# One held indirect transfer per recurrence step, and the low half of hs on VectorE

## The chip, the cores and the metric

The kernel runs on one core of a Trainium2 chip. The metric is the device time of one execution in microseconds (us). Three executions of the kernel before took 518.39, 520.9 and 521.04 us, a median of 520.9 us.

## The reference

For 32 sequences of 128 tokens with 256 features, the reference computes two gated blocks.

```python
# block 1: q = layernorm(x), k = v = context; 16 heads of 16
r = decay * r + kt * vt
inp = (qt * r) @ Wi.T + bi
gate = sigmoid(inp @ Wg.T + bg)
state = tanh((gate * state + (1 - gate) * inp) @ A.T + inp @ Bm.T)
out = state @ Wo.T + bo                    # x = x + tanh(g) * out
# block 2: fx = layernorm(x), 8 experts, top 2 of a softmax
shared = swiglu(fx @ w_shared_in) @ w_shared_out
hid = swiglu(fx @ w1_shared)
routed = sum over e of weight[:, e] * (hid @ w2[e])
x = x + tanh(g) * (shared + routed)
```

`state` depends on the state one token earlier, so 128 recurrence steps follow each other whatever else is done.

## The kernel before

The 128 tokens are cut into 16 tiles of 8 tokens (STEPS = 8), which for 32 sequences are 256 rows each. Five engines run programs of their own, written out by hand and held together by semaphores. Iteration i of every engine's program contains the eight recurrence steps of tile i and, in the eight slots behind them, parts of the work on neighbouring tiles: the input projections of tile i + 1, the output projection of tile i - 1, and the second block of tile i - 2. Iteration i runs from 1 to 18; the last recurrence is in iteration 15, so iterations 16 to 18 are a tail without one. Below, "step (i, t)" is step t of tile i.

One step is a ring of three engines. TensorE (PE) multiplies the high and the low half of `u` with A (L590, then L595) and raises `sum_done`. ScalarE (ACT) waits for that and computes the tanh (`tanh_step`, L959), which raises `st_ready`. VectorE (DVE) waits for that and makes `u_hi`, `u_full` and `u_lo` of the next step (`gated_state`, L1268 to L1273). Each engine runs its instructions in order, so whatever stands in a slot in front of the next step delays it if it is not done.

hs is the hidden tile of the shared expert. DVE makes it in slot 1 (L1597), ACT rounds it to the high half (L1160), and GpSimd (POOL) subtracts to make the low half (L1766), which PE needs for the product with w_shared_out in slot 3 (L576, `so_hi`, `hs_lo`). In the last tile alone, DVE makes that low half, in slot 2 (`low`, L1228).

The routed experts of tiles 0 to 11 are done in three chunks of four tiles. The rows of `hid` are kept in `hid_rows` and sent to DRAM (`hrows`), sorted by expert, by indirect DMAs that POOL issues (`scatter`, L1823, 16 a chunk, 128 rows each). When all 16 of a chunk have landed (`scattered`), SyncE (SP) issues DMA transposes that bring them back two blocks at a time (`turn_rows`, L473), PE multiplies each pair with its expert's w2 (`duo`, L623), ACT moves the product to SBUF (L1126), SP stores it to `yrows` (L483), and indirect DMAs of POOL fetch each token's rows (`gather`, L1836, 16 a chunk), which DVE adds up (L1298, L1306). Tiles 12 to 15 are dense: all eight experts for each token, in `pair` products (L576 with `hid_hi`, `hid_lo`) on PE.

AT lists the iteration and slot of each of the 36 duos, 12 a chunk; START is the iteration of each chunk's first one: 8, 12 and 15. SP issues a chunk's first four transposes at the end of its iteration START - 1; the others are issued one by one as duos are stored. POOL issues its indirect DMAs at two spots of an iteration, 0 at its start, behind a wait for tanh (i, 0), and 1 at its end, with no wait. The SCATTERS and GATHERS plans give 2 to 5 of them to a spot up to iteration 15. In between stand hs's low half, the reciprocal roots of both layernorms (`x_rstd`, L1773, and L1876) and hid's low half (L1766).

Of the kernel before, what the change touches and what calls it, by code (L numbers as in the profile page):

```python
# [50 lines left out]
STEPS = 8  # L51
# [52 lines left out]
def gated_layer(nc, x, ctx_in, g_xattn, g_ffn, Wi, bi, Wg, bg, A, Bm, Wo, bo, decay,  # L104
                w_shared_in, w_shared_out, w1_shared, w2, w_gate, gate_bias, out):
    with ExitStack() as stack:
# [276 lines left out]
        def run(eng, iteration):  # L383

            for i in range(1, LAST):
                iteration(i, first)

        AT = ([(i, slot) for i in (8, 9, 10, 12) for slot in (0, 2, 3, 5)] + [(13, slot) for slot in (0, 1, 2, 3, 5)]
              + [(14, slot) for slot in (0, 1, 2)] + [(15, 5)] + [(16, slot) for slot in range(5) for _ in range(2)] + [(16, 5)])
        DUOS = {}  # L390
        for n, at in enumerate(AT):
            DUOS.setdefault(at, []).append(n)
# [3 lines left out]
        def duo_bank(n, i, slot):  # L396

            if i < TILES:
                return bank[3 if slot == 5 and first.dense(i - 2) else {0: 5, 1: 3, 2: 5, 3: 4, 5: 5}[slot]][:, :]
            return flat(rec[n % 2][:, :, :])  # L400

        def duo_chunk(n):
# [134 lines left out]
        def _(pe):  # L537
# [256 lines left out]
            def duos_at(i, slot):  # L794

                for n in DUOS.get((i, slot), ()):
                    if n == 0:
                        pe.wait_ge(w2_lo, E)
                    if i >= TILES:
                        pe.wait_ge(st_ready, STEPS * TILES)  # L800
                        if AT[n - 2][0] >= TILES:
                            pe.wait_ge(y_ready, n - 1)
                    elif slot == 0:
                        if (i - 1, 5) in DUOS:
                            pe.wait_ge(y_ready, evacuated(i - 1, 5))
                    elif slot == 1:
                        pe.wait_ge(lg_ready, i - 1)
                    elif slot == 2:
                        pe.wait_ge(y_ready, evacuated(i, 0))
                    elif slot == 3:  # L810
                        pe.wait_ge(x1_ready, i)
                    elif first.dense(i - 2):
                        pe.wait_ge(lg_ready, i - 1)
                    else:
                        pe.wait_ge(y_ready, evacuated(i, 2))
                    duo(n, duo_bank(n, i, slot))

            def iteration(i, k):
# [103 lines left out]
                if k.has(c):  # L922
                    for q in range(len(CHUNKS)):
                        if d == last_of(q):
                            pe.wait_ge(routing, 7 * (q + 1))
                    if k.has(d):
                        pe.wait_ge(hid_ready, k.n(d))
                    else:
                        pe.wait_ge(ret_ready, k.n(1))
                    if k.dense(d):  # L930
                        pe.wait_ge(pair_used[1], k.nth(d))
                    feature_product(bank[B_SHB], "sh", xn2_s[c % 2], True, col=D).then_inc(sh_done, 1)
                    if c == 0:
                        pe.wait_ge(wide_lo, 2)
                    if k.has(a):
                        pe.wait_ge(gt_ready, k.n(a))
                    else:
                        pe.wait_ge(lg_ready, k.n(d))
                        pe.wait_ge(y_ready, evacuated(15, 5))

                    for s in range(HALVES):
                        for kc in range(KC):
                            for v in xn2_s[c % 2]:
                                last = pe.matmul(bank[B_LG][:, s * 2 * E:(s + 1) * 2 * E], v[:, kc, s * P:(s + 1) * P],
                                                 wgate_s[:, kc, :], start=(s == 0 and kc == 0 and v is xn2_s[c % 2][0]),
                                                 stop=(kc == KC - 1 and v is xn2_s[c % 2][1]), skip_group_check=True)
                    last.then_inc(lg_done, 1)
# [278 lines left out]
        def _(dve):  # L1226
# [346 lines left out]
            def iteration(i, k):  # L1573
# [44 lines left out]
                if k.has(d):  # L1618
                    dve.wait_ge(w1_done, k.n(d))
                    dve.wait_ge(sil_w_ready, k.n(d))  # L1620
                    if k.has(d - 1):
# [1 line left out]
                        dve.wait_ge(hid_lo, k.n(d - 1))  # L1623
                    dve.scalar_tensor_tensor(out=flat(hid[:, :, :]), in0=bank[B_W1B][:, :], scalar=hid_in[:, 1:2],
                                             in1=flat(sil_w[:, :, :]), op0=ALU.mult, op1=ALU.mult).then_inc(hid_ready, 1)
                if d == TILES - 1:
                    dve.wait_ge(hs_hi, k.n(d))
                    dve.wait_ge(so_done, k.n(d - 1))
                    low(flat(hs_s[1][:, :, :]), flat(hs[:, :, :]), flat(hs_s[0][:, :, :]), hs_lo)
                if k.has(f):  # L1630
                    dve.wait_ge(ln1_stats, k.n(f))
# [126 lines left out]
        def _(pool):  # L1758
# [6 lines left out]
            def low(n, whole, hi, signal):  # L1765
                pool.tensor_tensor(n, whole, hi, ALU.subtract).then_inc(signal, 1)  # L1766
# [78 lines left out]
                for row, at in zip(rows, spots, strict=True):  # L1845
                    plan.setdefault(at, []).append(row)

            spread(SCATTERS, range(0, 4), [(5, 1)] * 2 + [(6, 0)] * 3 + [(6, 1)] * 4 + [(7, 0)] * 4 + [(7, 1)] * 3)
            spread(SCATTERS, range(4, 8), [(9, 1)] * 2 + [(10, 0)] * 3 + [(10, 1)] * 4 + [(11, 0)] * 4 + [(11, 1)] * 3)
            spread(GATHERS, range(0, 4), [(12, 0)] * 4 + [(12, 1)] * 5 + [(13, 0)] * 5 + [(13, 1)] * 2)  # L1850
            spread(SCATTERS, range(8, 12), [(13, 1)] * 3 + [(14, 0)] * 4 + [(14, 1)] * 5 + [(15, 0)] * 4)
            spread(GATHERS, range(4, 8), [(15, 1)] * 4 + [(16, 0)] * 4 + [(16, 1)] * 8)
            spread(GATHERS, range(8, 12), [(17, 1)] * 16)

            def moves(i, spot):

                if spot == 0 and i < TILES and ((i, 0) in SCATTERS or (i, 0) in GATHERS):
                    pool.wait_ge(st_ready, STEPS * i + 1)
                for t, s, pick in SCATTERS.get((i, spot), ()):
                    scatter(t, s, pick)  # L1860
                for t, s, pick in GATHERS.get((i, spot), ()):
                    gather(t, s, pick)

            def iteration(i, k):
                c, d, f = i - 1, i - 2, i + 2

                moves(i, 0)
                if k.has(d) and d < TILES - 1:
                    pool.wait_ge(hs_hi, k.n(d))
                    if k.has(d - 1):  # L1870
                        pool.wait_ge(so_done, k.n(d - 1))
                    low(flat(hs_s[1][:, :, :]), flat(hs[:, :, :]), flat(hs_s[0][:, :, :]), hs_lo)
                x_rstd(f, k)
                if k.has(c):
                    pool.wait_ge(ln2_var, k.n(c))
                    pool.tensor_tensor(rs2[c % 2][:, :], ve2[c % 2][:, :], minus_half[:, :], ALU.pow).then_inc(ln2_rstd, 1)  # L1876
                    pool.wait_ge(ln2_rstd, k.n(c))
                    pool.tensor_tensor(nr2[c % 2][:, :], nm2[c % 2][:, :], rs2[c % 2][:, :], ALU.mult).then_inc(ln2_shift, 1)
                if k.has(d) and d < TILES - 1:
# [40 lines left out]
```

## Time and profile before

| | us |
|---|---|
| median of three executions | 520.9 |
| the profiled execution | 519.97 |
| its span, first to last instruction | 518.2 |
| PE busy | 434.6 (84% of the span) |
| DVE busy | 364.1 |
| ACT busy | 221.7 |
| POOL busy | 184.9 |
| mean granted TensorE clock, as a share of full speed | 0.962 |

The chain of work that ended last goes 46% through PE, 24% through DVE, 5% through ACT and 2% through POOL; 10% of it is "issue", time in which the engine waited for nothing that the profile shows, and 7% is "another core or an unknown queue", although the program runs on one core. Idle time is put down to whatever released the engine; "remote" there is a releaser that the profile could not name.

### The profile page before, as it was taken

The numbers are of one execution on the slowest core, as the hardware profiler recorded it, in microseconds if no ns is written. First come the engines' busy times: TensorE is split into PE (matmuls) and PEld (weight loads), VectorE is DVE, ScalarE is ACT, GpSimd is POOL, SyncE is SP. The second block draws the span as 40 slices with busy tenths as digits, with TensorE's granted clock in tenths as the row PEclk, the third lists the DMA queues.
The fourth block names the chain that finished last, engine by engine and source line by source line (L and its number), as shares of the span: only waits on it lengthen the run. The fifth ranks groups of instructions, "written<-read, shape, count | busy, mean of one in ns | idle before, by whom it ended". The sixth has DMA issues, their size and how long they took to land.

```text
span 518.2 us, 12156 instructions
## 1 busy us (share of the span) xinstructions
PE 434.6 (84%) x4324; PEld 355.5 (69%) x4324; DVE 364.1 (70%) x1303; ACT 221.7 (43%) x520; POOL 184.9 (36%) x225
## 2 busy tenths in 40 slices
PE   5977799999997959999988898879869979968660
PEld 4965688878885748898877777778756747645320
DVE  3687887989797857777776775767837865406865
ACT  3655555667564625464545444536232313212100
POOL 3012302224136374111154554442454370520632
PEclk9998899999999998999999999999989989979986
DMA  7783234052251221874642349647331365832424
GB/s 162 209 222 111 41 104 119 15 144 45 101 135 52 63 82 38 168 123 113 132 115 96 99 97 180 143 129 128 123 103 52 81 154 134 200 113 73 139 80 148
DMA packets 102571, 59.14 MB, mean 114 GB/s; under 512 B 74352, under 2 KB 92784, under 8 KB 102512
## 3 DMA queue, kind: packets, MB, share of 16 engines
q1 hardware_dynamic: 97776, 45.77, 36.7%
q0 software_dynamic: 4736, 12.59, 7.9%
q8 instruction: 36, 0.59, 0.5%
q14 instruction: 23, 0.19, 0.1%
HBM read 23.74 MB, written 25.56 MB: 95 GB/s over the span
## 4 chain that ended last, share of the span: by engine, by line
PE 46%; DVE 24%; issue 10%; another core or an unknown queue 7%; ACT 5%; POOL 2%; DMA 1%; POOLq 0%; DVEq 0%; ACTq 0%
PE bank L576 12%; PE bank L565 10%; PE bank L623 5%; PE rec L709 5%; PE rec L590 4%; DVE u_hi L1268 4%; PE rec L623 3%; PE rec L595 2%; DVE u_full L1270 2%; DVE r L1371 2%; PE rec L565 1%; PE bank L842 1%; ACT state L959 1%; DVE ret L1384 1%
## 5 line engine op out<-in xcount | busy, mean ns | idle before, releaser
L959 ACT ACTIVATE state<-rec 128x64 f32<-128x64 f32 x128 | 36.6, 286 | 183.6 <-PE rec L595 138.5
L1268 DVE SCALAR_TENSOR_TENSOR u_hi<-gt,state 128x64 f16<-128x64 f32 x127 | 44.6, 351 | 86.7 <-ACT state L959 73.5
L590 PE MATMUL rec<-u_hi,a_hi 128*128 128x32 f16 x512 | 48.8, 196 | 28.4 <-DVE u_hi L1268 20.5
L1836 POOL DMA_INDIRECT yg<-yrows,slots_i x48 | 49.6, 1034 | 56.0 <-issue 35.5
L1823 POOL DMA_INDIRECT hrows<-hid_rows,slots_i x48 | 49.8, 1037 | 53.6 <-issue 25.3
L590 PEld LDWEIGHTS rec<-u_hi,a_hi 128*128 128x128 f16 x512 | 37.5, 99 | 38.0 <-DVE u_hi L1268 25.9
L590 PE MATMUL rec<-u_hi,a_lo 128*128 128x32 f16 x512 | 48.3, 195 | 1.0 <-issue 1.0
L1766 POOL TENSOR_TENSOR hs_lo<-hs,hs_hi 128x512 f16<-128x512 f32 x15 | 17.4, 1163 | 72.4 <-ACT hs_hi L1160 71.6
L590 PEld LDWEIGHTS rec<-u_hi,a_lo 128*128 128x128 f16 x512 | 35.9, 99 | 3.7 <-issue 1.8
L595 PE MATMUL rec<-u_lo,a_hi 128*128 128x32 f16 x512 | 36.8, 196 | 1.5 <-issue 0.5
L565 PE MATMUL bank<-xn_hi,sh_hi 128*128 128x256 f16 x128 | 34.9, 273 | 0.0
L565 PE MATMUL bank<-xn_hi,sh_lo 128*128 128x256 f16 x128 | 34.9, 273 | 0.0
L565 PE MATMUL bank<-xn_lo,sh_hi 128*128 128x256 f16 x128 | 34.9, 273 | 0.0
L1773 POOL TENSOR_TENSOR rs<-ve,minus_half 128x2 f32<-128x2 f32 x16 | 12.3, 772 | 60.6 <-DVE nm L1439 60.6
L1270 DVE SCALAR_TENSOR_TENSOR u_full<-gt,state 128x64 f32<-128x64 f32 x127 | 33.7, 266 | 0.0
L1273 DVE TENSOR_TENSOR u_lo<-u_full,u_hi 128x64 f16<-128x64 f32 x127 | 30.4, 240 | 4.4
L576 PE MATMUL bank<-w_hi,hid_hi 128*128 128x512 f16 x64 | 25.3, 395 | 9.6 <-DVE raw_w L1289 4.1
L842 PE MATMUL bank<-whole_wo,state 128*128 128x256 f32 x128 | 32.6, 400 | 0.0
L576 PE MATMUL bank<-w_hi,xn_hi 128*128 128x256 f16 x96 | 26.3, 274 | 6.5 <-DVE hs L1597 6.2
L709 PE MATMUL rec<-cn,whole_a 128*128 128x256 f32 x128 | 31.4, 388 | 0.2 <-DVE cn L1405 0.2
L1286 DVE SCALAR_TENSOR_TENSOR raw_w<-bank,wts,raw_w 128x256 f32<-128x256 f32 x32 | 15.4, 480 | 22.7 <-PE bank L576 16.2
L595 PEld LDWEIGHTS rec<-u_lo,a_hi 128*128 128x128 f16 x512 | 23.7, 99 | 5.1 <-DVE u_lo L1273 3.2
(291 smaller groups left out, 1419.6 us busy)
## 6 DMA issues: line engine op xcount, KB each, us to landing
yrows<-squares_sh SPq DMA_DIRECT2D x18, 256.0 KB
x_sb<-in_x_dram SPq DMA_DIRECT2D x16, 256.0 KB, 3.3
c_sb<-in_ctx_dram SPq DMA_DIRECT2D x64, 64.0 KB
xr_sb<-in_x_dram SPq DMA_DIRECT2D x16, 256.0 KB
hrows<-zeros SPq DMA_DIRECT2D x4, 1024.0 KB, 5.7
yrows<-squares_w SPq DMA_DIRECT2D x15, 256.0 KB
raw_w<-in_L_ffn_w_dram SPq DMA_DIRECT2D x8, 256.0 KB, 4.4
out_dram<-raw_w SPq DMA_DIRECT2D x8, 256.0 KB
```

The lines of the kernel that those rows point to most:

```text
L565: last = pe.matmul(o, w[:, kc, at], a[:, kc, :], start=first, stop=(kc == KC - 1 and w is w_lo), skip_group_check=True)
L576: last = pe.matmul(dst, a[:, kc, s * P:(s + 1) * P], w(part, kc), start=first, stop=(kc == KC - 1 and a is a_lo), skip_group_check=True)
L590: pe.matmul(o[:, oc, :], w[:, kc, oc * P:(oc + 1) * P], u_hi[t % 2][:, kc, :], start=False, stop=False, skip_group_check=True)
L595: last = pe.matmul(o[:, oc, :], a16[0][:, kc, oc * P:(oc + 1) * P], u_lo[t % 2][:, kc, :], start=False, stop=(kc == KC - 1), skip_group_ch ...
L623: last = pe.matmul(dst[:, b * D:(b + 1) * D], hid_t[n % RING][:, half * KC + kc, b * P:(b + 1) * P], split["w2"][part][:, kc, bass.ds(e, 1 ...
L709: last = pe.matmul(rec[a % 2][:, oc, :], whole_a[:, kc, oc * P:(oc + 1) * P], cn[a % 2][:, kc, :], start=False, stop=(kc == KC - 1), skip_ ...
L842: last = pe.matmul(bank[B_WO][:, s * D:(s + 1) * D], state[c % 2][:, kc, s * P:(s + 1) * P], whole_wo[:, kc, :], start=False, stop=(kc == ...
L959: act.activation(step_of(state[i % 2], t), step_of(rec[i % 2], t), ACT.Tanh, scale=1.0 / PSCALE).then_inc(st_ready, 1)
L1268: dve.scalar_tensor_tensor(out=u_hi[p][:, :, :], in0=gate, scalar=1.0, in1=old, op0=ALU.add, op1=ALU.mult).then_inc(uh_ready, 1)
L1270: dve.scalar_tensor_tensor(out=u_full[p][:, :, :], in0=gate, scalar=1.0, in1=old, op0=ALU.add, op1=ALU.mult).then_inc(uf_ready, 1)
L1823: pool.indirect_dma_start(hrows[q % 2], bass.IndirectOffsetOnAxis(ap=slots_i[q][:, at:at + 1], axis=0), hid_rows[t % 6][:, s, :, :].rearra ...
L1836: pool.indirect_dma_start(yg[t % 4][:, s, pick, :], None, yrows[q % 2], bass.IndirectOffsetOnAxis(ap=slots_i[q][:, at:at + 1], axis=0), bo ...
```

## The change

The low half of hs is made by DVE in slot 2 of every tile, behind hid, and no more by POOL. POOL's indirect DMAs stand in eight spots of an iteration, one for each step, and up to iteration 15 each spot has one of them and waits for its step's tanh. The rows of the plan move: scatters of chunk 0 from iterations 5 to 7 to iterations 6 and 7, of chunk 1 from 9 to 11 to 10 and 11, of chunk 2 from 13 to 15 to 14 and 15; gathers of chunk 0 stay in 12 and 13; gathers of chunk 1 go from 15 and 16 to 16 alone, two a spot; gathers of chunk 2 stay in 17. The first duo of chunk 2 moves from (15, 5) to (16, 0), so START becomes 8, 12 and 16, and two waits that it needed go.

```diff
-              + [(14, slot) for slot in (0, 1, 2)] + [(15, 5)] + [(16, slot) for slot in range(5) for _ in range(2)] + [(16, 5)])
+              + [(14, slot) for slot in (0, 1, 2)] + [(16, slot) for slot in range(6) for _ in range(2)])
...
-                return bank[3 if slot == 5 and first.dense(i - 2) else {0: 5, 1: 3, 2: 5, 3: 4, 5: 5}[slot]][:, :]
+                return bank[{0: 5, 1: 3, 2: 5, 3: 4, 5: 5}[slot]][:, :]
...
-                    elif first.dense(i - 2):
-                        pe.wait_ge(lg_ready, i - 1)
...
-                        pe.wait_ge(y_ready, evacuated(15, 5))
...
-                if d == TILES - 1:
+                if k.has(d):
                     dve.wait_ge(hs_hi, k.n(d))
-                    dve.wait_ge(so_done, k.n(d - 1))
+                    if k.has(d - 1):
+                        dve.wait_ge(so_done, k.n(d - 1))
                     low(flat(hs_s[1][:, :, :]), flat(hs[:, :, :]), flat(hs_s[0][:, :, :]), hs_lo)
...
-            spread(SCATTERS, range(0, 4), [(5, 1)] * 2 + [(6, 0)] * 3 + [(6, 1)] * 4 + [(7, 0)] * 4 + [(7, 1)] * 3)
-            spread(SCATTERS, range(4, 8), [(9, 1)] * 2 + [(10, 0)] * 3 + [(10, 1)] * 4 + [(11, 0)] * 4 + [(11, 1)] * 3)
-            spread(GATHERS, range(0, 4), [(12, 0)] * 4 + [(12, 1)] * 5 + [(13, 0)] * 5 + [(13, 1)] * 2)
-            spread(SCATTERS, range(8, 12), [(13, 1)] * 3 + [(14, 0)] * 4 + [(14, 1)] * 5 + [(15, 0)] * 4)
-            spread(GATHERS, range(4, 8), [(15, 1)] * 4 + [(16, 0)] * 4 + [(16, 1)] * 8)
-            spread(GATHERS, range(8, 12), [(17, 1)] * 16)
+            def slots(*iterations, each=1):
+                return [(i, t) for i in iterations for t in range(STEPS) for _ in range(each)]
+            spread(SCATTERS, range(0, 4), slots(6, 7))
+            spread(SCATTERS, range(4, 8), slots(10, 11))
+            spread(GATHERS, range(0, 4), slots(12, 13))
+            spread(SCATTERS, range(8, 12), slots(14, 15))
+            spread(GATHERS, range(4, 8), slots(16, each=2))
+            spread(GATHERS, range(8, 12), slots(17, each=2))
-            def moves(i, spot):
-                if spot == 0 and i < TILES and ((i, 0) in SCATTERS or (i, 0) in GATHERS):
-                    pool.wait_ge(st_ready, STEPS * i + 1)
+            def moves(i, t):
+                if i < TILES and ((i, t) in SCATTERS or (i, t) in GATHERS):
+                    pool.wait_ge(st_ready, STEPS * i + t + 1)
...
                 moves(i, 0)
-                if k.has(d) and d < TILES - 1:
-                    pool.wait_ge(hs_hi, k.n(d))
-                    if k.has(d - 1):
-                        pool.wait_ge(so_done, k.n(d - 1))
-                    low(flat(hs_s[1][:, :, :]), flat(hs[:, :, :]), flat(hs_s[0][:, :, :]), hs_lo)
+                moves(i, 1)
+                moves(i, 2)
                 x_rstd(f, k)
+                moves(i, 3)
                 if k.has(c):
                     pool.wait_ge(ln2_var, k.n(c))
...
                         low(hid_rows[d % 6][:, :, 1, :], hid[:, :, :], hid_rows[d % 6][:, :, 0, :], hid_lo)
+                moves(i, 4)
                 if 3 <= i <= 6:
                     w2_low(2 * (i - 3))
                     w2_low(2 * (i - 3) + 1)
-                moves(i, 1)
+                for t in range(5, STEPS):
+                    moves(i, t)
```

## Rows read from the trace of the kernel before

**Rows 1.** The waits: engine and line, releaser, total us, times, longest us.

```profile
ACT state L959 <- remote: 38.7, 10, 7.8
```

**Rows 2.** Windows, from tanh (i, 0) to tanh (i + 1, 0); last, the tail.

```profile
core 0: us, PE busy (x) PEld busy (x) DVE busy (x) ACT busy (x) POOL busy (x), PEclk, DMA share, GB/s
112.68:134.12 21.44, 19.86 (x226) 17.10 (x225) 18.42 (x68) 13.65 (x33) 6.66 (x8) 1.00 0.33 91
...
155.62:181.34 25.72, 20.71 (x228) 17.36 (x227) 19.89 (x71) 13.79 (x33) 13.05 (x14) 1.00 0.22 58
181.34:209.70 28.36, 21.56 (x224) 18.39 (x222) 18.61 (x68) 11.35 (x28) 16.35 (x18) 0.88 0.25 70
209.70:233.67 23.97, 23.93 (x275) 21.76 (x273) 17.82 (x68) 13.03 (x33) 4.07 (x6) 1.00 0.77 139
...
366.47:403.20 36.73, 30.20 (x283) 23.47 (x281) 23.00 (x83) 10.47 (x27) 18.44 (x18) 0.95 0.25 84
403.20:431.80 28.60, 24.24 (x206) 16.02 (x204) 19.90 (x73) 6.57 (x17) 15.35 (x16) 0.94 0.48 122
431.80:518.20 86.40, 58.68 (x376) 36.58 (x374) 47.12 (x136) 13.46 (x26) 27.95 (x28) 0.89 0.45 128
```

**Rows 3.** Timeline of step (7, 2), beside eight scatters: start, duration, engine, line.

```profile
182.63 1.07 POOL L1823 DMA_INDIRECT hrows<-hid_rows,slots_i  x1 [0.17 <-issue]
...
187.08 0.28 PE L595 MATMUL rec<-u_lo,a_hi 128*128 128x32 f16 x4
...
191.98 0.28 ACT L959 ACTIVATE state<-rec 128x64 f32<-128x64 f32 x1 [5.80 <-remote]
```

**Rows 4.** Timeline of step (13, 1), beside five gathers.

```profile
337.41 1.02 POOL L1836 DMA_INDIRECT yg<-yrows,slots_i  x1 [5.86 <-ACT state L959]
...
338.95 0.28 PE L595 MATMUL rec<-u_lo,a_hi 128*128 128x32 f16 x4
...
341.90 0.28 ACT L959 ACTIVATE state<-rec 128x64 f32<-128x64 f32 x1 [4.77 <-remote]
```

**Rows 5.** Timeline of steps (15, 0) and (15, 1): a transfer held for its tanh.

```profile
403.20 0.29 ACT L959 ACTIVATE state<-rec 128x64 f32<-128x64 f32 x1 [1.12 <-PE rec L595]
404.28 0.97 POOL L1823 DMA_INDIRECT hrows<-hid_rows,slots_i  x1 [8.78 <-ACT state L959]
...
405.78 0.28 PE L595 MATMUL rec<-u_lo,a_hi 128*128 128x32 f16 x4
...
406.36 0.29 ACT L959 ACTIVATE state<-rec 128x64 f32<-128x64 f32 x1 [0.68 <-PE rec L595]
```

**Rows 6.** Windows of 2 us in tile 7, after PE's idle time.

```profile
195.00:197.00 2.00, 2.00 (x12) 1.38 (x11) 1.93 (x10) 1.49 (x5) 0.77 (x1) 0.50 0.00 0
```

**Rows 7.** Timeline: chunk 1's last scatter, its first transposes, its first duo.

```profile
302.70 0.98 POOL L1823 DMA_INDIRECT hrows<-hid_rows,slots_i  x1 [0.30 <-issue]
...
305.13 2.60 SPq L473 DMA_TRANSPOSE raw_sh<-hrows  x2
...
309.60 0.28 PE L623 MATMUL bank<-w_hi,raw_sh 128*128 x1 [0.57 <-issue]
```

**Rows 8.** The chain in order of time, at step (8, 0): start, us, what.

```profile
207.63 0.12 PE rec L595 x4
...
209.60 1.31 PE bank L576 x12
```

**Rows 9.** Timeline of tile 4, slots 2 and 3, and DVE's low half in tile 15.

```profile
120.62 0.27 PE L576 MATMUL bank<-so_hi,hs_hi 128*128 128x256 f16 x1
120.92 0.28 ACT L959 ACTIVATE state<-rec 128x64 f32<-128x64 f32 x1
121.64 0.27 DVE L1268 SCALAR_TENSOR_TENSOR u_hi<-gt,state 128x64 f16<-128x64 f32 x1
...
483.29 0.68 DVE L1228 TENSOR_TENSOR hs_lo<-hs,hs_hi 128x512 f16<-128x512 f32 x1
```

**Rows 10.** Timeline: the first pair product of tile 13, in iteration 15.

```profile
416.88 0.40 PE L576 MATMUL bank<-w_hi,hid_hi 128*128 128x512 f16 x1 [2.26 <-POOL hid_lo L1766]
```

More of the change, by code:

```diff
@@ L1846, in spread @@
                     plan.setdefault(at, []).append(row)
-            spread(SCATTERS, range(0, 4), [(5, 1)] * 2 + [(6, 0)] * 3 + [(6, 1)] * 4 + [(7, 0)] * 4 + [(7, 1)] * 3)
-            spread(SCATTERS, range(4, 8), [(9, 1)] * 2 + [(10, 0)] * 3 + [(10, 1)] * 4 + [(11, 0)] * 4 + [(11, 1)] * 3)
-            spread(GATHERS, range(0, 4), [(12, 0)] * 4 + [(12, 1)] * 5 + [(13, 0)] * 5 + [(13, 1)] * 2)
-            spread(SCATTERS, range(8, 12), [(13, 1)] * 3 + [(14, 0)] * 4 + [(14, 1)] * 5 + [(15, 0)] * 4)
-            spread(GATHERS, range(4, 8), [(15, 1)] * 4 + [(16, 0)] * 4 + [(16, 1)] * 8)
-            spread(GATHERS, range(8, 12), [(17, 1)] * 16)
-            def moves(i, spot):
-                if spot == 0 and i < TILES and ((i, 0) in SCATTERS or (i, 0) in GATHERS):
-                    pool.wait_ge(st_ready, STEPS * i + 1)
[L1859 to L1862, printed above, removed]
+            def slots(*iterations, each=1):
[9 more added lines that the diff above has]
+                    pool.wait_ge(st_ready, STEPS * i + t + 1)
+                for row in SCATTERS.get((i, t), ()):
+                    scatter(*row)
+                for row in GATHERS.get((i, t), ()):
+                    gather(*row)
             def iteration(i, k):
```

## The prediction

> **What bounds the kernel now.** I read the page first: PE is busy 84% of the span, yet 7% of the chain that ended last is put down to an unknown queue, in a program on one core. The waits say where: ten times ACT's tanh waits for a releaser without a name, 38.7 us in all, 7.8 at the longest [rows 1]. Then I cut the span at every tanh (i, 0) [rows 2]. Tile 4, with no indirect DMA and no duo, takes 21.44 us. Tile 8, with four duos and no indirect DMA, takes 23.97 with PE busy for 23.93: it is bound by PE. Tiles 6 and 7 have no duos, and take 25.72 and 28.36.
>
> The timeline shows what is late. In step (7, 2) PE's last matmul ends at 187.08 + 0.28 = 187.36, and the tanh that waits for nothing else starts at 191.98, 4.62 us later, while POOL issues eight scatters back to back from 182.63 on [rows 3]. Beside gathers, step (13, 1): PE done at 339.23, tanh at 341.90, 2.67 us late [rows 4]. Elsewhere the same handoff takes 0.04 us. Going through all 128 steps I find 20 that are late by over 0.1 us, the first (6, 2) by 2.59, the last (15, 6) by 0.11, the longest (14, 2) by 5.35; they sum to 32.7 us, and every one stands in or just behind a run of indirect DMAs.
>
> PE then idles, and its clock falls: from 195 to 197 the granted clock is 0.50 [rows 6], that is 1.2 GHz of 2.4, after 5 us without a matmul. The means of tiles 7, 14 and 15 are 0.88, 0.95 and 0.94 [rows 2], so length times the missing share is 3.4, 1.8 and 1.7 us lost, 2.3 a time.
>
> **The change part by part.**
>
> *Runs of transfers go.* Late handoffs 32.7 and clock 6.9 make 39.6 us. Not all of it is on the path: tile 7 over tile 4 is 6.9 us and tile 6 over it 4.3, where handoffs and clock alone would say 9.7 and 2.6. I take 37, with 30 to 41 as ends.
>
> *One transfer is left in each step*, 64 of them in eight tiles (6, 7, 10 to 15). A held transfer starts 1.08 us after its tanh and takes 0.97 [rows 5]. In that row the next sum was ready at 406.06, 1.78 us into it, with a second one just begun, and the tanh came at 406.36, 0.30 late. Signals due 0.5 to 0.75 us after the first transfer of a run were on time; those due 1.4 to 2.0 us after the last one came through 2.0 to 2.3 us after its start. So I read a transfer as closing the handoff from about 1 to 2.1 us after its start. Steps are 1.5 to 4 us apart, so signals fall due 0.7 to 2.9 us into a lone transfer; two or three of eight are caught, for 0.2 to 1.1 us. I take 1.7 us a tile, +14; ends 0 (each passes) and 30 (gathers hold as in [rows 4]: four runs of gathers let the tanh through only 4.3 to 4.5 us after their first start).
>
> *The first duo of each chunk waits.* This is what spreading costs. A chunk's last scatter now waits for the last tanh of tiles 7, 11 and 15, and SP's transposes wait for it. Before, the last scatter of chunk 1 started at 302.70, the transposes at 305.13, and the first duo at 309.60 after 0.57 us of idle time [rows 7]: 2.43 plus 4.47. With 1.08 in front, the first duo can start 7.98 us after the last tanh. PE finished that step's sum at 207.75 and would reach duo 0 at 209.60 + 1.31 = 210.91 [rows 8], 3.1 us after the tanh. So PE stands 4.9 us at (8, 0), and 4.9 less the old 0.57 at (12, 0). Tile 8 has no slack to take it [rows 2], and after 5 us of idle time I add the 2.3 for the clock each time: 4.9 + 4.3 + 4.6 = +14. Ends 9 (clock holds) and 18.
>
> *The tail.* At (16, 0) PE comes at 2.6 us and stands 5.4; the clock adds 2. Moved duo 24 adds 1.3, taken from tile 15. Eight gathers that stood in tile 15 now run behind the last scatter with no hold; they delay the evacuations of the first duos, but PE stands anyway. Against that, the ring of four transposes fills once more. Following PE through the slots of iteration 16 I find it 8 us later at its last duo: +8 here, -1 in tile 15. The tail of 86.40 us [rows 2] is else unchanged. Ends 3 and 14.
>
> *The low half of hs.* On DVE it takes 0.68 us [rows 9], some 0.6 net of overlap. In tile 4, slot 2 is full on DVE: tanh (4, 3) starts at 120.92 and ends at 121.20, and `u_hi` starts at 121.64 only, behind that slot's work. So 0.6 us goes onto the path. PE, which starts on `hs_lo` at 120.62 [rows 9], would have it at 121.9, and that delay is inside the same 0.6 or 0.7. Tiles 2 to 7, 11 and 15 make 8 x 0.65 = +5. In tiles bound by PE, DVE ends the low half before PE asks: 0. What POOL loses, 1.16 us a tile, was beside idle time of DVE: 0. Ends 2 and 10 (every tile).
>
> *POOL's order.* The transfer of slot 3 stands before the roots of the second layernorm and hid's low half, and holds them some 0.7 us in tiles 6, 7 and 11, where the chain goes through them. In tile 15 PE waited 2.26 us for hid's low half [rows 10]: +1. Together +3, ends 0 and 6; elsewhere PE is the bound and hides it.
>
> The sum: -37 + 14 + 14 + 8 - 1 + 5 + 3 = +6 us. The profiled execution took 519.97 us, 1.8 outside its span, so about 526, 5 above the median of 520.9.
>
> By the Trainium skill's page SBUF — State Buffer, section "Who interferes with whom", DMA never contends with a compute engine and PE and ACT never wait on anyone; then the late handoffs would have another cause and the first term would not exist. This trace disagrees in its timing: 20 late of 20 beside transfers.
>
> **The rivals.**
>
> *A. Lone transfers pass every signal and the clock holds.* For it: signals 0.5 to 0.75 us into a run were on time. Against it: the 0.30 of [rows 5], and the clock of [rows 6]. Then -37 + 0 + 9 (the duos without the clock) + 6 (the tail without it) - 1 + 5 + 3 = -15, so about 505; with only one of the two, 512 to 519. This is the other side: it decides as soon as held transfers cost under 0.05 us each. I weigh it at its middle, 514.
>
> *B. The hold doesn't hold.* POOL is one queue: behind the waits for layernorm and hid in slots 3 and 4, transfers bunch with gaps of 0.30 us. Runs of two or three lost 0.4 to 1 us before. Five tiles with such a run add 5 us: 531.
>
> *C. Gathers are the poison.* Each of 16 held gathers holds its tanh some 2 us more: 526 + 16 x 1.5 = 550. For it, four of four runs; against it, in those the second gather began 1.4 us in.
>
> *D. The cause is another one*, as the page's rule would have it: nothing of 37 goes, and 14 for lone transfers doesn't come: 526 + 23 = 549. The coincidence of 20 in 20 speaks against it.
>
> **How the numbers follow.** Forecast (the sum) 0.45, its own range 519 to 533; A 0.28; B 0.15; C 0.08; D 0.04. Under 0.5%, 2.6 us, a measurement can't tell it from no change. Faster: A nearly whole and a little of the forecast, 0.29. Same, 518.3 to 523.5: a third of the forecast and a bit of A, 0.18. Slower: 0.53. The range 508 to 539 leaves out C, D and the far end of A.
>
> **What would show it.** Right: PE idle for about 5 us in front of L623 at (8, 0), (12, 0) and (16, 0), a clock of 0.5 behind each; tiles 7 and 14 some 5 to 8 us shorter, tiles 8 and 12 longer; in plain tiles 0.6 us more between tanh 3 and 4 or 4 and 5. Wrong: late tanhs of 2 us and more beside lone transfers (C), no `remote` waits and no idle time before the first duos (A), or the old waits at new places (D).

## The result, and the profile after

The changed kernel takes 537.25 us (median; 534.4 to 538.8), the kernel before 520.97 beside it on the same chip: a ratio of 1.0321, 95% interval 1.0269 to 1.0373. It is slower, as forecast, by 16.3 us where the sum said about 5: outside the 519 to 533 that the forecast gave itself, and near the far end of 508 to 539, the range over all rivals. The profiled execution has a span of 537.1 against 518.2.

The windows of the changed kernel, again from tanh (i, 0) to tanh (i + 1, 0), for tiles 4, 6, 7, 8, 12, 14, 15 (to its last tanh, tanh (15, 7)) and the tail, with the columns of [rows 2]:

```profile
113.78:135.89 22.11, 19.66 (x226) 17.14 (x225) 19.04 (x69) 13.73 (x33) 5.46 (x7) 1.00 0.33 90
158.04:185.14 27.10, 21.73 (x228) 18.46 (x227) 21.74 (x72) 13.62 (x34) 11.55 (x13) 0.94 0.21 55
185.14:211.54 26.40, 22.04 (x224) 18.68 (x222) 18.73 (x69) 11.55 (x29) 15.54 (x17) 0.87 0.15 51
211.54:243.75 32.21, 25.63 (x275) 22.62 (x273) 18.33 (x69) 13.02 (x33) 4.15 (x6) 0.89 0.65 124
314.33:346.82 32.49, 26.23 (x281) 23.13 (x279) 19.83 (x72) 13.12 (x32) 13.02 (x14) 0.89 0.75 154
374.02:405.40 31.38, 29.14 (x288) 23.11 (x286) 23.12 (x86) 10.48 (x26) 11.32 (x12) 1.00 0.24 81
405.40:432.52 27.12, 22.05 (x188) 13.67 (x187) 19.33 (x72) 5.95 (x16) 8.99 (x10) 0.94 0.14 49
432.52:537.10 104.58, 67.95 (x388) 40.29 (x386) 47.68 (x137) 14.03 (x27) 35.14 (x36) 0.82 0.49 130
```

Read against [rows 2], tile 4 is 0.67 longer, tile 7 2.0 and tile 14 5.4 shorter, tile 8 8.2 longer, and PE's clock in tile 8 has gone from 1.00 to 0.89. The last tanh stands at 432.52, before at 431.80: over all sixteen tiles the change is nearly even. The tail is 18.2 longer. That is the result.

The waits answer [rows 1]: of ten tanh waits without a named releaser one is left.

```profile
ACT state L956 <- remote: 3.7, 1, 3.7
```

The one is step (7, 2) again, where the hold did not keep the transfers apart. The timeline of PE, ACT and POOL, to be read against [rows 3]:

```profile
187.75 0.98 POOL L1821 DMA_INDIRECT hrows<-hid_rows,slots_i  x1 [0.30 <-ACT state L956]
...
190.31 0.97 POOL L1821 DMA_INDIRECT hrows<-hid_rows,slots_i  x1 [0.30 <-issue]
...
190.86 0.28 PE L595 MATMUL rec<-u_lo,a_hi 128*128 128x32 f16 x4
...
193.64 0.28 ACT L956 ACTIVATE state<-rec 128x64 f32<-128x64 f32 x1 [3.68 <-remote]
```

PE is done with the sum at 190.86 + 0.28 = 191.14 and the tanh starts at 193.64, 2.50 late, within a run of five transfers. Over all 128 steps the late handoffs (over 0.1 us) sum to 5.8 us in 12; the same count of the kernel before gives 32.9 in 21.

The first duo of chunk 0, where [rows 7] had 0.57 us of idle time for chunk 1:

```profile
210.69 2.08 POOL L1821 DMA_INDIRECT hrows<-hid_rows,slots_i  x1 [2.70 <-ACT state L956]
...
214.23 2.69 SPq L473 DMA_TRANSPOSE raw_sh<-hrows  x2
...
219.28 0.39 PE L623 MATMUL bank<-w_hi,raw_sh 128*128 x1 [6.53 <-issue]
```

PE stands 6.53 us. The window behind it shows the slow clock of [rows 6] again:

```profile
216.00:222.00 6.00, 2.72 (x16) 2.05 (x17) 0.00 (x0) 0.00 (x0) 0.00 (x0) 0.50 1.00 189
```

The tail falls into three stretches, cut at POOL's first gather of chunk 2 and of chunk 3. Windows of the kernel before, then of the changed one:

```profile
431.80:479.37 47.57, 40.63 (x292) 28.48 (x290) 19.72 (x61) 12.10 (x23) 11.28 (x12) 0.93 0.51 133
479.37:499.51 20.14, 13.71 (x74) 6.68 (x72) 16.91 (x52) 1.35 (x3) 8.55 (x9) 1.00 0.29 93
499.51:518.20 18.69, 4.34 (x12) 1.41 (x12) 10.49 (x25) 0.00 (x0) 8.13 (x8) 0.67 0.45 154
```

```profile
432.52:490.92 58.40, 44.29 (x303) 30.82 (x302) 20.10 (x62) 12.68 (x24) 19.15 (x20) 0.88 0.63 152
490.92:518.47 27.55, 18.36 (x75) 7.87 (x73) 17.16 (x52) 1.35 (x3) 8.01 (x9) 0.81 0.21 67
518.47:537.10 18.63, 5.30 (x12) 1.60 (x12) 10.42 (x25) 0.00 (x0) 7.98 (x8) 0.61 0.47 155
```

The first grew by 10.8 us, the second by 7.4 with the same work in it, its clock from 1.00 to 0.81. In the second, gathers run back to back, and VectorE waits three times for a releaser without a name, where the products that it reads come from PE (timeline of the changed kernel):

```profile
494.15 0.27 PE L565 MATMUL bank<-xn_hi,w_lo 128*128 128x256 f16 x1
...
496.14 1.00 POOL L1834 DMA_INDIRECT yg<-yrows,slots_i  x1 [0.30 <-issue]
496.24 0.75 DVE L1621 SCALAR_TENSOR_TENSOR hid<-bank,hid_in,sil_w 128x512 f32<-128x512 f32 x1 [2.06 <-remote]
...
499.82 0.48 DVE L1283 SCALAR_TENSOR_TENSOR raw_w<-bank,wts,raw_w 128x256 f32<-128x256 f32 x1 [1.46 <-remote]
...
502.77 0.75 DVE L1662 SCALAR_TENSOR_TENSOR raw_w<-bank,out_un,x 128x512 f32<-128x512 f32 x1 [1.95 <-remote]
```

The last matmul for `hid` ends at 494.42, and VectorE's instruction starts at 496.24, 1.82 late. It is the lateness of [rows 3], on VectorE.

### The profile page after: what moved, and what is told of

Its sections match the earlier page's. It is cut to its first block, busy times and chain, and to the rows that moved or that the text cites. A ratio compares the mean times of both kernels' runs of the same rounds, so it can differ in the third digit from the quotient of the medians.

```text
span 537.1 us, 12154 instructions
## 1 busy us (share of the span) xinstructions
PE 443.3 (83%) x4324; PEld 360.0 (67%) x4324; DVE 372.3 (69%) x1318; ACT 221.5 (41%) x520; POOL 171.2 (32%) x210
## 4 chain that ended last, share of the span: by engine, by line
PE 52%; DVE 25%; issue 8%; another core or an unknown queue 4%; ACT 3%; DMA 1%; POOL 1%; DVEq 0%; POOLq 0%; ACTq 0%
PE bank L576 14%; PE bank L565 10%; PE bank L623 6%; PE rec L709 5%; PE rec L590 4%; DVE u_hi L1265 4%; PE rec L623 3%; PE rec L595 2%; PE bank L840 2%; PE rec L565 2%; DVE u_full L1267 2%; ACT state L956 2%; DVE r L1368 2%; DVE hid L1621 1%
## 5 line engine op out<-in xcount | busy, mean ns | idle before, releaser
L1265 DVE SCALAR_TENSOR_TENSOR u_hi<-gt,state 128x64 f16<-128x64 f32 x127 | 40.6, 320 | 83.9 <-ACT state L956 82.0
L1821 POOL DMA_INDIRECT hrows<-hid_rows,slots_i x48 | 54.8, 1143 | 80.8 <-ACT state L956 60.3
L590 PEld LDWEIGHTS rec<-u_hi,a_hi 128*128 128x128 f16 x512 | 37.7, 99 | 25.2 <-DVE u_hi L1265 22.0
L1771 POOL TENSOR_TENSOR rs<-ve,minus_half 128x2 f32<-128x2 f32 x16 | 12.3, 769 | 124.7 <-DVE nm L1436 124.7
L1283 DVE SCALAR_TENSOR_TENSOR raw_w<-bank,wts,raw_w 128x256 f32<-128x256 f32 x32 | 15.4, 481 | 35.9 <-PE bank L576 26.9
L576 PE MATMUL bank<-w_hi,hid_hi 128*128 128x512 f16 x64 | 27.9, 435 | 10.7 <-DVE raw_w L1286 9.8
L1270 DVE TENSOR_TENSOR u_lo<-u_full,u_hi 128x64 f16<-128x64 f32 x127 | 32.8, 258 | 4.3
L709 PE MATMUL rec<-cn,whole_a 128*128 128x256 f32 x128 | 32.8, 401 | 0.0
L623 PE MATMUL bank<-w_hi,raw_sh 128*128 x96 | 20.3, 297 | 13.2 <-issue 7.0
L576 PE MATMUL bank<-so_hi,hs_hi 128*128 128x256 f16 x64 | 18.1, 282 | 13.8 <-DVE hs_lo L1225 13.8
```

Source lines behind the costliest of these rows:

```text
L576: last = pe.matmul(dst, a[:, kc, s * P:(s + 1) * P], w(part, kc), start=first, stop=(kc == KC - 1 and a is a_lo), skip_group_check=True)
L590: pe.matmul(o[:, oc, :], w[:, kc, oc * P:(oc + 1) * P], u_hi[t % 2][:, kc, :], start=False, stop=False, skip_group_check=True)
L623: last = pe.matmul(dst[:, b * D:(b + 1) * D], hid_t[n % RING][:, half * KC + kc, b * P:(b + 1) * P], split["w2"][part][:, kc, bass.ds(e, 1 ...
L709: last = pe.matmul(rec[a % 2][:, oc, :], whole_a[:, kc, oc * P:(oc + 1) * P], cn[a % 2][:, kc, :], start=False, stop=(kc == KC - 1), skip_ ...
L1265: dve.scalar_tensor_tensor(out=u_hi[p][:, :, :], in0=gate, scalar=1.0, in1=old, op0=ALU.add, op1=ALU.mult).then_inc(uh_ready, 1)
L1821: pool.indirect_dma_start(hrows[q % 2], bass.IndirectOffsetOnAxis(ap=slots_i[q][:, at:at + 1], axis=0), hid_rows[t % 6][:, s, :, :].rearra ...
```

## The experiments

"Stretch A" is from tanh (15, 7) to the first gather of chunk 2, "stretch B" from there to the first gather of chunk 3; the rest is 18.5 to 18.9 us in every kernel. (The rivals A and B of the prediction have nothing to do with these.) "Late" is the sum (and count) of tanh handoffs over 0.1 us. Times are medians, ratios are to the kernel before on the same chip in the same session; its own median was 520.97 beside the changed kernel, then 522.9 for e1 to e4, 524.3 for e5 to e8 and 522.8 for e9 to e12. The ratios are not quotients of the medians and differ from them by up to 0.004. The last four columns are from one profiled execution of each kernel, which can lie up to 3.3 us from its median.

| kernel | us | ratio | tanh (15, 7) | late | stretch A | stretch B |
|---|---|---|---|---|---|---|
| before | 521.0 | 1 | 431.8 | 32.9 (21) | 47.6 | 20.1 |
| changed | 537.3 | 1.032 | 432.5 | 5.8 (12) | 58.4 | 27.6 |
| e1_low_dve | 541.2 | 1.032 | 448.7 | 37.7 (20) | 47.4 | 26.8 |
| e2_held_low_pool | 523.4 | 1.000 | 424.7 | 6.1 (8) | 56.9 | 20.2 |
| e3_early | 524.5 | 1.003 | 426.8 | 15.4 (18) | 48.9 | 26.6 |
| e4_pairs | 547.1 | 1.045 | 441.2 | 12.3 (20) | 58.7 | 24.9 |
| e5_early_low_pool | 512.4 | 0.977 | 420.5 | 15.4 (13) | 49.4 | 20.1 |
| e6_spaced_gathers | 529.9 | 1.012 | 431.5 | 6.8 (14) | 58.5 | 19.7 |
| e7_shifted_gathers | 534.0 | 1.014 | 434.0 | 6.3 (13) | 59.3 | 23.8 |
| e8_low14_pool | 536.8 | 1.022 | 432.5 | 6.5 (13) | 58.6 | 24.9 |
| e9_singles | 508.2 | 0.971 | 416.3 | 13.7 (12) | 49.8 | 20.1 |
| e10_singles_spaced | 500.4 | 0.955 | 417.8 | 14.5 (14) | 42.6 | 20.0 |
| e11_singles_dve | 523.1 | 1.001 | 426.0 | 20.4 (20) | 51.3 | 24.9 |
| e12_before_spaced | 538.8 | 1.027 | 445.2 | 5.8 (14) | 45.9 | 28.2 |

**The two halves of the change, each alone.** e1_low_dve is the kernel before with only VectorE's edit:

```
-                if d == TILES - 1:
+                if k.has(d):
                     dve.wait_ge(hs_hi, k.n(d))
...
```

(and `hs_lo`'s three lines taken off POOL). e2_held_low_pool is the changed kernel with those lines back on POOL, between `moves(i, 1)` and `moves(i, 2)`, and VectorE's only for the last tile.

> The kernel before with one edit: VectorE makes the low half of hs in slot 2 of every tile, GpSimd never. Transfers as before. My term: 0.65 us in each of tiles 2 to 7, 11 and 15, where slot 2 of VectorE is full, nothing elsewhere: +5, 526 us. The traces of before and after already show +0.66 to +0.75 in tiles 2 to 5. Rival: beside the runs of transfers GpSimd's subtraction stood in VectorE's way (u_hi took 1.67 us behind the run in tile 7), so taking it away gives back 1 to 1.5 us in five tiles: 518 to 521 us.

> The changed kernel with the low half of hs back on GpSimd, between the transfers of steps 1 and 2. If the two parts of the change add, it is 5 us faster than the changed one: 532 us. Rival: in GpSimd's queue the low half now stands behind a transfer held for tanh 1, TensorE's shared-expert product waits for it, and nothing is gained: 537 us.

Both missed, e1 by 15 us and e2 by 9. The ratios are 1.0321 (1.0264 to 1.0379) and 1.0004 (0.9971 to 1.0037): held transfers alone change nothing in the sum (7.1 us won up to tanh (15, 7), 9.3 lost in stretch A), and the low half alone costs as much as the whole change (18.3 us by the medians). How it costs, e1's timeline of step (11, 3) shows:

```profile
303.05 0.28 ACT L959 ACTIVATE state<-rec 128x64 f32<-128x64 f32 x1 [0.65 <-PE rec L595]
303.90 0.68 DVE L1228 TENSOR_TENSOR hs_lo<-hs,hs_hi 128x512 f16<-128x512 f32 x1
304.73 0.37 PE L576 MATMUL bank<-so_hi,hs_hi 128*128 128x256 f16 x1 [1.72 <-DVE hs_lo L1228]
304.92 0.27 DVE L1268 SCALAR_TENSOR_TENSOR u_hi<-gt,state 128x64 f16<-128x64 f32 x1
...
307.03 0.42 PE L576 MATMUL bank<-so_hi,hs_lo 128*128 128x256 f16 x1
307.24 0.26 PE L590 MATMUL rec<-u_hi,a_hi 128*128 128x32 f16 x1
...
308.03 0.29 ACT L959 ACTIVATE state<-rec 128x64 f32<-128x64 f32 x1 [3.28 <-PE rec L595]
```

and the same step in the kernel before:

```profile
294.20 0.27 PE L576 MATMUL bank<-so_hi,hs_hi 128*128 128x256 f16 x1
294.40 0.29 ACT L959 ACTIVATE state<-rec 128x64 f32<-128x64 f32 x1 [0.69 <-PE rec L595]
...
295.99 0.20 PE L590 MATMUL rec<-u_hi,a_hi 128*128 128x32 f16 x1 [0.32 <-DVE u_hi L1268]
...
296.76 0.29 ACT L959 ACTIVATE state<-rec 128x64 f32<-128x64 f32 x1 [0.65 <-PE rec L595]
```

Before, the `so` product ran while ACT made the tanh. Now it waits for `hs_lo`, which VectorE makes after that tanh, and its twelve matmuls (here at half clock, 0.21 us apart for 0.11) stand in PE's queue ahead of the next recurrence product: 4.98 us from tanh to tanh for 2.36. Taken over all tiles, step 3 to step 4 is 14.0 us longer in e1 than before, and 12.5 longer in the changed kernel than in e2: 1.2 in each of tiles 2 to 6 and 11, 2.7 and 1.7 in tiles 7 and 15, 0.1 to 0.2 in tiles 8 to 10, 12 and 13, with a part given back in the next steps (7.8 net at tanh (15, 7)). That 7.8 is a low figure: e2's tile 1, which has no low half yet, happened to be 1.9 us longer (24.4 for 22.6). From tile 2 on the difference is 10.3 us.

**Where the transfers stand.** e3_early is the changed kernel with a chunk's last eight scatters two a step, ending at step 3; e4_pairs has all sixteen two a step in the second tile, ending at step 7. Of each, the line of chunk 0's plan (first e3's, then e4's); those of chunks 1 and 2 change in the same way:

```
-            spread(SCATTERS, range(0, 4), slots(6, 7))
+            spread(SCATTERS, range(0, 4), slots(6) + [(7, t) for t in range(4) for _ in range(2)])
...
+            spread(SCATTERS, range(0, 4), slots(7, each=2))
```

> The changed kernel, but each chunk's last eight scatters go two a step behind steps 0 to 3 of its second tile, so that the last has landed before the next tile begins. Theory: the idle time of 6.5 us before the first duos at (8, 0), (12, 0) and (16, 0), and the slow clock behind it, came from the last scatter being held for the tile's last tanh. Then 8 + 7 us go from tiles 8 and 12 and 8 to 9 from the tail, and the pairs cost 1 to 3 us in each of three tiles: 518 us, 514 to 522. Rival: the transposes themselves keep TensorE waiting, or what is saved at (16, 0) is lost again to the runs of gathers in the tail: 530 us or more.

> The changed kernel, but all 16 scatters of a chunk go two a step in its second tile (7, 11 and 15), none in the first. It counts what a run of two costs against lone ones. If each transfer closes the handoff from TensorE to ScalarE until some 2.1 us after its start, a run of two closes it until 3.4 us, and nearly every step of three tiles is late by 0.5 to 1 us: +12 to +18 against the changed kernel less the 2 to 3 us that the lone scatters cost: 548 us. Rival: only runs of three and more hold it: 537 us, within 2.

e3's interval is 0.9994 to 1.0067, e4's 1.0405 to 1.0499. With e3, tiles 8 and 12 fall from 32.2 and 32.5 us to 24.1 and 24.8 and stretch A from 58.4 to 48.9: 25.3 us that were the first duo's wait and what followed from it. It gives back 9.3 in tiles 7, 11 and 15, since pairs merge into runs (late from 5.8 to 15.4). With 1 to 3 us a tile expected for the pairs (6 in all at the middle), that accounts for some 3 of the 6 us by which e3 ended above its expectation; the rest is open. e4's 547.1 is what was expected, though for a mixed reason: late handoffs grew by 6.5 us only, to 12.3 in 20 steps, and tiles 8 and 12 by 1.6 each.

**Both terms out.**

> The changed kernel with both terms taken out at once: the last eight scatters of each chunk stand two a step behind steps 0 to 3 of its second tile, and the low half of hs is on GpSimd again. Theory (the two terms are separate and add): e2_held_low_pool had tiles 8 and 12 at 32.4 and 33.2 us, e3_early had them at 24.1 and 24.8, and e3's way from tanh(15,7) to the first gather of chunk 2 was 48.9 us against 56.9. From e2's 523.4: -8.3 for tile 8, -8.4 for tile 12, -8 at (16,0), +5 for the pairs in tile 7 and +5 for tile 15 (e3 against the changed kernel), so about 508 to 511, faster than both kernels. Rival (what is cut out of the recurrence comes back in the tail, because GpSimd's gathers meet TensorE's signals again): 518 to 521.

Measured 512.4 (510.3 to 516.1), interval 0.9695 to 0.9845: 1.4 above the expected 508 to 511 and far below the rival's 518. Within this spread the two terms add as the theory says. One signal, at (7, 2), is 5.4 us late: pairs had merged into a run of seven.

**Stretch B.** e6 and e7 are the changed kernel with a GpSimd instruction whose result nobody uses, in e6 behind each of the first seven gathers of iteration 17 (chunk 2), in e7 once ahead of the first. e6:

```
                 for row in GATHERS.get((i, t), ()):
                     gather(*row)
+                    if i == 17 and row[0] in (8, 9) and row != (9, 1, 1):
...
+                        pool.tensor_tensor(spare[:, at:at + 2], ve2[1][:, :], minus_half[:, :], ALU.pow)
```

e7: `pool.wait_ge(combined, 5)` and one `ALU.mult` ahead of `gather(8, 0, 0)`. e8 makes tile 14's low half on POOL (`if k.has(d) and d == 14`) and the others on VectorE.

> The changed kernel, with a GpSimd power of 128x2 (about 0.8 us, its result unused) behind each of the first seven gathers of chunk 2. Theory (TensorE's signals are late only within a run of transfers 0.3 us apart): VectorE's three waits of 2.06, 1.46 and 1.95 us shrink to below 0.7 each, and the 27.5 us from the first gather of chunk 2 to the first of chunk 3 become 21 to 23; time 531 to 533. Rival (these waits have nothing to do with the gathers, or with their spacing): 27 to 28 us and 537, or more, as the run of gathers is 6 us longer.

> The changed kernel, with one GpSimd multiply of 128x2 (about 0.2 us and 0.1 of gap, its result unused) between the wait and the first gather of chunk 2, so that the run starts about 0.3 us later against TensorE. The kernel before started it 3.21 us ahead of the end of the L565 group that hid waits for, the changed kernel about 3.5. Theory (whether a signal is late hangs on where in the run it falls): the 27.5 us become 20 to 21, time 530 to 531. Rival (the 7 us come from the low half of tile 14 on VectorE, whose kernels were all slow there and whose rivals all fast): 27 to 28 us, time 537.

> The changed kernel with the low half of hs of tile 14 alone on GpSimd, between the transfers of steps 1 and 2 of iteration 16; VectorE makes the others. Theory of position (a run's place against TensorE decides): only a shift by chance; the low half itself lies 40 us ahead of the stretch, so 27 to 28 us from gather to gather, time about 536 to 537. Rival (the low half of tile 14 on VectorE costs the tail 7 us): 20 us, time about 530.

In e6 stretch B is 19.7 us, all three late waits are gone, and the clock is 1.00; its time is 529.9, interval 1.0073 to 1.0166. In its timeline `hid` starts after 0.29 us of idle time, released by PE by name:

```profile
491.94 1.07 POOL L1835 DMA_INDIRECT yg<-yrows,slots_i  x1 [0.19 <-issue]
493.04 0.72 POOL L1868 TENSOR_TENSOR spare<-ve,minus_half 128x2 f32<-128x2 f32 x1
493.53 0.75 DVE L1622 SCALAR_TENSOR_TENSOR hid<-bank,hid_in,sil_w 128x512 f32<-128x512 f32 x1 [0.29 <-PE bank L566]
493.94 1.07 POOL L1835 DMA_INDIRECT yg<-yrows,slots_i  x1 [0.18 <-issue]
```

Eight gathers now take 15.5 us in place of 10.1, and stretch B is 7.9 us shorter. So the spacing matters for VectorE's waits too. e7's run started 0.9 us later rather than 0.3 (the multiply took 0.36 and a gap of 0.5 followed): two of three late waits went, the third (2.20) stayed, and stretch B is 23.8, short of the 20 to 21 expected. In e8 stretch B is 24.9, where its theory expected 27 to 28 and its rival 20: both missed, and the low half of tile 14 alone does not decide it.

What goes with it in all fourteen kernels is where the run stands against VectorE. The first gather starts at 479.37 before and at 490.92 in the changed kernel (the windows above), and VectorE's next `lg_b`, first in the timeline of before, then of the changed kernel, 0.48 and 0.78 us later:

```profile
479.85 0.23 DVE L1581 SCALAR_TENSOR_TENSOR lg_b<-bank,in_un,gb_all 128x16 f32<-128x16 f32 x1
```

```profile
491.70 0.23 DVE L1578 SCALAR_TENSOR_TENSOR lg_b<-bank,in_un,gb_all 128x16 f32<-128x16 f32 x1
```

At 0.48 (before, e2, e5, e9) stretch B is 20.1 or 20.2 in all four; at 0.77 or 0.78 with an unspaced run (changed, e1, e3, e4, e8, e11, e12) it is 24.9 to 28.2; at 0.77 with a spaced run (e6, e10) 19.7 and 20.0; e7 has 0.67 and 23.8. What shifts the run by 0.3 us stays open: e12 has the low half on POOL and 28.2, so it is not that edit as such.

**Singles and spacing.** e9_singles is e5 with one scatter a step, three of them moved ahead into tile 5 (9, 13); e10 adds the power behind each gather of tiles 4 to 9; e11 is e9 with the low half on VectorE:

```
+            spread(SCATTERS, range(0, 4), [(5, 5), (5, 6), (5, 7)] + slots(6) + [(7, t) for t in range(5)])
...
+                    if 4 <= row[0] < 10:
...
+                        pool.tensor_tensor(spare[:, at:at + 2], unit[:, :], minus_half[:, :], ALU.pow)
```

> The kernel with early scatters and the low half on GpSimd (512.4), its pairs taken apart: the 16 scatters of a chunk stand one a step, from step 5 of the tile before through step 4 of the second tile. Theory (a lone transfer delays a signal by under 0.8 us, and the pairs alone made tiles 7, 11 and 15 30.2, 26.1 and 27.4 us long, of which signals late by 15.4 us in all): tiles 7, 11 and 15 fall to 24.2, 21.1 and 24.5 us as in e2_held_low_pool, tiles 5, 9 and 13 grow by under 1 us each, so 12 us less: about 500 to 502. Rival (scatters issued before the first tile's end slow that tile as much as the pairs slowed the last): 508 to 512.

> e9_singles, with a GpSimd power of 128x2 (about 0.8 us, result unused) behind each gather of tiles 4 to 9, those of iteration 16 and the first eight of iteration 17. Theory (signals are late within runs 0.3 us apart): in e5_early_low_pool ACT's squares_w started at 447.87, 6.2 us after the end of its last matmul at 441.71, with five gathers between; this goes, and the first gather of chunk 2 comes 4 to 6 us earlier after tanh(15,7) than in e9. The next stretch has no late signal in e5 (20.1 us) and stays at 20. So 4 to 6 us under e9, 495 to 498. Rival (ACT waited there for something that the transfers only accompany, or the 6 us are not on the path): as e9, or 1 us over it.

> e9_singles with the low half of hs on VectorE in every tile, as in the changed kernel: the low half's cost in a kernel without runs. Theory (two prices: 0.66 us in a tile in which TensorE is busy throughout, 1.2 to 2.7 us from step 3 to step 4 in tiles 6, 7, 11 and 15, in which the product that waits for the low half slips behind the sum of step 3): 8 to 10 us more than e9 up to tanh(15,7), 0 to 7 more behind it, according to where VectorE's waits fall in the run of chunk 2's gathers (20.1 or 26 to 27.5 us). So 509 to 518. Rival (the prediction's 0.65 x 8 = 5 us): 505 to 507.

e9 took 508.2 us, where the rival had 508 to 512: tiles 7, 11 and 15 fell to 24.2, 21.1 and 24.3, as the theory said, but tiles 6, 10 and 14 grew from 25.0, 23.7 and 30.8 in e5 to 28.2, 25.3 and 35.9. POOL reached the transfers meant for tile 5 only in tile 6 (timeline; tanh (6, 0) is at 156.53):

```profile
156.70 1.15 POOL L1763 TENSOR_TENSOR w_lo<-raw_w,w_hi 128x512 f16<-128x512 f32 x1 [7.35 <-DVE packed L1350]
158.03 2.03 POOL L1820 DMA_INDIRECT hrows<-hid_rows,slots_i  x1 [0.18 <-issue]
...
164.21 0.97 POOL L1820 DMA_INDIRECT hrows<-hid_rows,slots_i  x1 [0.30 <-issue]
```

It had waited 7.35 us for VectorE's `packed`, the holds had passed by the time it came to each transfer, and five went as one run. A hold for a tanh sets a transfer's earliest start, and no distance to the one ahead of it.

e10 is the fastest, 500.4 us, interval 0.9503 to 0.9603, 7.8 under e9 where 4 to 6 were expected. ACT's `squares_w`, which in e5 waited 10.76 us and started 6.2 us after PE's last matmul for it (441.44 + 0.27), starts in time. Timeline of e5, then of e10:

```profile
441.44 0.27 PE L623 MATMUL rec<-w_hi,raw_w 128*128 x1
...
447.87 1.07 ACT L1123 COPY squares_w<-rec 128x512 f32<-128x512 f32 x2 [10.76 <-remote]
```

```profile
438.31 0.27 PE L626 MATMUL rec<-w_hi,raw_w 128*128 x1
438.62 0.58 ACT L1126 COPY squares_w<-rec 128x512 f32<-128x512 f32 x1 [0.72 <-PE rec L626]
```

Stretch A is 42.6 us, 7.2 less than in e9, with a clock of 1.00. The kernel before has the same wait, 10.8 us, and the changed one 10.3.

e11 is 14.9 over e9: 9.6 up to tanh (15, 7), as expected, 1.5 in stretch A and 4.8 in stretch B. The prediction's 5 us for the low half are ruled out a second time.

**The spacing alone, in the kernel before.** A power behind every transfer up to tile 15, nothing else:

```
+                pool.tensor_tensor(spare[:, at:at + 2], unit[:, :], minus_half[:, :], ALU.pow)
```

> The kernel before, with a GpSimd power of 128x2 (about 0.8 us, result unused) behind each of its transfers up to tile 15: same transfers, same places, no hold, only 1 us apart in place of 0.3. Theory (what delays TensorE's signals is a run 0.3 us apart, not a transfer as such): the late signals, 32.9 us in 21 handoffs over 0.1 us, fall below 10 us; against that the runs of seven and eight last 6 us longer and can delay GpSimd's own work at the head of a tile; tanh(15,7) at 400 to 415 in place of 431.8, time 500 to 512. Rival (the delay goes with each transfer, or with the time during which transfers are under way): late signals 30 us or more, 521 to 530.

Late handoffs fall from 32.9 to 5.8, as the theory says; yet it is 16 us slower (interval 1.0213 to 1.0332), which neither side expected. The profiled executions, 20 us apart, differ by 13.4 us up to tanh (15, 7), and by 8.0 in stretch B, whose gathers are not spaced here. The first of the two has a cause that shows: a run of eight lasts 6 us longer, and POOL's low half stands behind it. Waits from 150 to 430 (PE has none for `hs_lo` there in the kernel before), and the timeline of step (7, 3), 14.22 us long:

```profile
PE bank L579 <- POOL hs_lo L1770: 34.2, 8, 10.9
```

```profile
193.62 0.28 ACT L962 ACTIVATE state<-rec 128x64 f32<-128x64 f32 x1 [0.95 <-PE rec L598]
201.39 1.04 POOL L1827 DMA_INDIRECT hrows<-hid_rows,slots_i  x1 [0.19 <-issue]
203.16 1.14 POOL L1770 TENSOR_TENSOR hs_lo<-hs,hs_hi 128x512 f16<-128x512 f32 x1
204.45 0.37 PE L579 MATMUL bank<-so_hi,hs_hi 128*128 128x256 f16 x1 [10.87 <-POOL hs_lo L1770]
...
207.84 0.29 ACT L962 ACTIVATE state<-rec 128x64 f32<-128x64 f32 x1 [12.65 <-PE rec L598]
```

## Why the prediction came out as it did

The direction was right, and the kinds of cost that it named are there. That up to tanh (15, 7) its terms sum to about -2 and the trace has +0.7 is luck in part: the first two terms were off by some 9 and 11 us and cancel. By its own steps:

- *Runs of transfers go (-37), lone transfers (+14).* Late handoffs went from 32.9 to 5.8, of which 2.5 are a run's. Lone transfers cost about 3 us, not 14. But the runs gave back less as well: of the 6.9 us for the clock nothing came, since the means of tiles 6, 7 and 15 are 0.94, 0.87 and 0.94 now, 6.7 us by the same count. With +1.0 in all from tile 2 to tanh (15, 7), 10.3 for the low half (against e2) and 15.8 for the first duos (tiles 8 and 12 against e3), -25 is left as an estimate for runs, lone transfers and all else, so about -28 for the runs, short of their 30 to 41. The prediction's own tile 7 pointed there: 6.9 us over tile 4, where handoffs and clock made 9.7. The reading that a transfer closes the handoff from 1 to 2.1 us after its start came mostly from signals inside runs; in e12, with 1 us between transfers, no tanh is over 1.1 us late.
- *The first duos (+14).* PE stood 6.53 us at (8, 0) and 6.21 at (12, 0), where 4.9 was worked out: the last scatter took 2.08 us, not 0.97, and the transposes 5.05 for 4.47. The clock fell to 0.50 each time. Tile 8 is 8.2 longer (7.2 forecast), and e3 gets 8.1 and 7.7 back in tiles 8 and 12: 15.8 for +14.
- *The low half of hs (+5).* Mis-sized. The step said that PE's delay is inside the 0.65 us that DVE loses. It is not: PE's product with `hs_lo` stands ahead of the ring's next step, and step 3 to step 4 grew by 1.2 us. In tiles 2 to 5 the next step gives 0.45 of it back, and the net of 0.66 to 0.75 agrees with the forecast all the same. In tiles 6, 7 and 15 the net is 2.1 to 2.7 (changed against e2); in tile 7 it falls at step 3, but in tile 6 1.4 of it at step 6, and in tile 15 3.8 at step 5 behind 2.8 less at step 4; why there, no run shows. So the low half costs 7.8 us up to tanh (15, 7), 10.3 from tile 2 on, and with both stretches 13.8 us by the medians (537.25 less 523.41), 3.2% by the ratios. Of this, 7.4 is stretch B, where the place of the run decides. Nearly the whole result hangs on this half, by way of the tail in part.
- *The tail (+8).* This is the term that failed: +18.2. Stretch A took 10.8, inside the term's ends of 3 and 14, for the reasons named: PE stood 6.68 us at (16, 0), the clock was 0.66 from 442 to 450, and e3 takes 9.5 of it away. Stretch B took 7.4 that no step named: "the tail is else unchanged" overlooked that its runs of gathers are the very runs of the first term, only meeting almost no signal there in the kernel before.
- *POOL's order (+3).* Not separated by any run.

The rivals: A had one half right (lone transfers nearly pass) and one wrong (the clock doesn't hold). B's 531 is the number nearest to the result, but not for its reason: it occurred once, at (7, 2), for 2.5 us. C did not occur: sixteen held gathers stand in tiles 12 and 13, which show no tanh over 0.75 us late. D is out: e6, e10 and e12 move the lateness by spacing the transfers. By the Trainium skill's page SBUF — State Buffer, section "Who interferes with whom", PE and ACT never wait on anyone. The section is about ports of SBUF; where it is read as saying that what PE hands to ACT comes in time beside a DMA, 32.9 us of late handoffs against 5.8 once the same transfers are spaced speak against it. By what path a run holds them back, no run shows. PE itself goes on: in e5 its next products start from 441.54, while ACT waits for the last one until 447.87. And since the profile's ends of matmuls are modelled, it could be the end of the product as well as its signal that is late.

## What to carry to other kernels

A chain of transfers with short gaps has a price at whatever waits for another engine's signal beside it, so look for waits without a named releaser and for the queue that is busy then. A distance of 1 us between transfers, here made with a GpSimd instruction of 0.72 us, removed most of it, and pays only if nothing due soon stands behind them in that queue (e12). Spreading work to the end of its slack moves the price to the first consumer: e3, e5 and e9 show that the last transfer's place is worth some 8 us a chunk. And an instruction moved to an engine with idle time on average can still put an in-order product of a third engine on the wrong side of a recurrence.

## What was not expected of the hardware

The position within the run matters: over all fourteen kernels, tanh signals due beside a lone transfer or the first of a run were at most 1.12 us late, beside later ones up to 5.4 (some of these came in time). The last scatter of chunks 0 and 1 took 2.08 us in place of 0.97, each started 0.05 us after VectorE's L1368, which has two inputs in SBUF; the first ran from 210.64 to 211.99. The last of chunk 2, with no such instruction beside it, took 0.97. All twelve indirect transfers over 1.3 us in the changed kernel start while an instruction of VectorE with two inputs in SBUF is under way; the reverse does not always hold (the one at 345.31, started 0.02 us after such an instruction, took 1.00). The Trainium skill's page SBUF — State Buffer, sections "SBUF: two separate sides" and "Who interferes with whom", says that an instruction of VectorE with two SBUF inputs contends with GpSimd's reads, and that the one that starts first holds the shared ports for its whole length; the 1.1 us here agree with it if an indirect transfer counts as such a read, and so does a gather of 1.52 us that started 0.03 us after `hs_lo` at 483.29 [rows 9]. The second of these sections infers that such an instruction does not hold back the making of a DMA's descriptors; these durations speak against that inference.
